# Router of two MoE layers: both halves of the split weights as one 64-column operand, and their sum taken in the turn to token rows

## What is computed

```
scores = sigmoid(x @ router_w.T)                 # f0: 8 columns, top 2 of 8
s      = sigmoid(xf @ Wr.T + br)                 # f1: 32 columns, top 6 of 32
x = x + tanh(g_ffn[0]) * _L0_ffn_ref(_layernorm(x), ...)
x = x + tanh(g_ffn[1]) * _L1_ffn_ref(_layernorm(x), ...)
```

## Time and profile before

| | |
|---|---|
| time, median of 3 | 902.48 us (901.77 to 905.25) |
| the profiled execution | 904.81 us, its span 902.9 us |
| TensorE matmul busy | 875.3 us, 97% of the span |
| VectorE busy | 600.3 us, 66% |
| ScalarE busy | 531.6 us, 59% |
| GpSimd busy | 133.6 us, 15% |
| mean granted TensorE clock | 0.992 |
| router matmuls (L369) | 48, of 8 or 32 stationary and 512 moving columns |
| turns back (L382) | 32 transposes |

### The profile page before, as it was taken

How to read it: one execution, slowest core, us unless ns; L and a number is a source line. 1 busy time by engine, 2 the same in 40 slices (tenths; PEclk the granted TensorE clock), 3 DMA queues, 4 the chain that set the end, 5 groups by cost and what they waited for, 6 DMA issues and landing times.

```text
span 902.9 us, 13884 instructions
## 1 busy us (share of the span) xinstructions
PE 875.3 (97%) x4747; PEld 716.1 (79%) x4768; DVE 600.3 (66%) x1228; ACT 531.6 (59%) x914; POOL 133.6 (15%) x112
## 2 busy tenths in 40 slices
PE   7898999999999999989999999999999999999997
PEld 7898887787788888767777777878788888888886
DVE  4998754466654565589999865658755466565564
ACT  3234343434554354457677767777677867777774
POOL 6996100001002020011121310000000000000000
PEclk9999999999999999999999999999999999999999
DMA  8230151444433442014333244434444344444433
GB/s 283 98 113 29 36 152 34 145 126 133 143 123 101 152 119 69 18 36 124 114 107 104 77 134 134 136 115 140 140 140 143 97 140 140 145 151 151 148 118 105
DMA packets 68389, 106.44 MB, mean 118 GB/s; under 512 B 9120, under 2 KB 31936, under 8 KB 67936
## 3 DMA queue, kind: packets, MB, share of 16 engines
q1 hardware_dynamic: 68112, 105.47, 37.1%
q10 hardware_dynamic: 208, 0.09, 0.0%
HBM read 96.79 MB, written 8.74 MB: 117 GB/s over the span
## 4 chain that ended last, share of the span: by engine, by line
PE 84%; DVE 7%; DMA 3%; POOL 2%; issue 2%; ACT 2%; SPq 1%; DVEq 0%; ACTq 0%; POOLq 0%
PE bank L685 38%; PE bank L721 29%; PE bank L1555 3%; PE bank L1566 2%; PE bank L1546 2%; PE bank L369 1%; PE bank L1458 1%; PE bank L1191 1%; PE bank L1190 1%; PE bank L1188 1%; DMA k_blocks<-k_parts 1%; PE bank L1575 1%; POOL pair_products L1058 1%; PE bank L1209 1%; DVE weighted L1279 1%
## 5 line engine op out<-in xcount | busy, mean ns | idle before, releaser
L482 ACT ACTIVATE y_hi<-y 128x512 fp32r<-128x512 f32 x200 | 124.1, 621 | 81.9 <-DVE y L565 81.2
L579 DVE TENSOR_TENSOR y<-y,gate_rows 128x512 f32<-128x512 f32 x124 | 85.8, 692 | 119.9 <-ACT y L471 118.5
L721 PE MATMUL bank<-y_hi,w_hi 128*128 128x512 f32 x400 | 157.3, 393 | 1.6 <-DVE y_lo L315 1.2
L721 PE MATMUL bank<-y_lo,w_hi 128*128 128x512 f32 x400 | 156.5, 391 | 0.0
L721 PE MATMUL bank<-y_hi,w_lo 128*128 128x512 f32 x400 | 156.0, 390 | 0.0
L315 DVE TENSOR_TENSOR y_lo<-y,y_hi 128x512 fp32r<-128x512 f32 x196 | 134.4, 686 | 29.9 <-ACT y_hi L482 29.6
L465 ACT ACTIVATE activated<-bank 128x512 f32<-128x512 f32 x136 | 81.1, 597 | 80.6 <-PE bank L685 75.8
L685 PE MATMUL bank<-x_hi_first,w_hi 128*128 128x512 f32 x264 | 106.2, 402 | 0.7 <-DVE w_lo L310 0.7
L685 PE MATMUL bank<-x_hi_first,w_lo 128*128 128x512 f32 x264 | 104.2, 395 | 0.0
L685 PE MATMUL bank<-x_lo_first,w_hi 128*128 128x512 f32 x264 | 104.1, 394 | 0.0
L685 PE MATMUL bank<-x_hi_last,w_hi 128*128 128x512 f32 x264 | 104.0, 394 | 0.0
(11 more groups left out here) (156 smaller groups left out, 1368.1 us busy)
## 6 DMA issues: line engine op xcount, KB each, us to landing
gate_rows<-gates SPq DMA_DIRECT2D x156, 256.0 KB, 3.7
w_raw<-in_wu SPq DMA_DIRECT2D x68, 256.0 KB, 2.6
w_raw<-in_wu SPq DMA_DIRECT2D x32, 384.0 KB, 4.1
k_blocks<-k_parts SPq DMA_DIRECT2D x128, 64.0 KB, 2.4
k_parts<-xn_split SPq DMA_DIRECT2D x32, 128.0 KB
v_slot<-in_v_rows SPq DMA_DIRECT2D x16, 256.0 KB, 2.7
ctx_windows<-in_ctx_win SPq DMA_DIRECT2D x3, 1024.0 KB, 13.7
x_mixed<-in_x SPq DMA_DIRECT2D x4, 512.0 KB, 9.3
```

Of the source, the lines that this page charges most:

```text
L482: act.activation(mem.yhi[:, K % S, :], mem.y[:, K % S, :], ACT.Copy).then_inc(s_yh, 1)
L579: dve.tensor_tensor(mem.y[:, K % S, :], mem.y[:, K % S, :], gate, ALU.mult).then_inc(s_yd, 1)
L721: last = pe.matmul(acc(s)[:, c, :], w_[:, Nu % S, wc], y_[:, K % S, :], start=(n == 0 and m == 0), stop=(n == U - 1 and m == 2), skip_grou ...
```

## The change

The router's stationary operand becomes one tile of 64 columns: the upper parts of the weights in columns 0 to 31, the lower parts in columns 32 to 63. For f0, which has 8 experts, the 8 columns are padded with zeros to 32 on the host. `logits_t` then makes four passes a block (x upper and x lower, for both halves of the contraction), so partitions 0 to 31 of the bank hold upper weights x (upper x + lower x), and partitions 32 to 63 lower weights x the same. (The product of both lower parts, left out before, is in it now.) The copy takes 64 partitions. `logits` is no transpose any more: it is a matmul in plain float32 whose moving operand `part_sum` is the 64 x 32 matrix of two identities one above the other (its first 8 columns for f0), which turns the block and adds its two parts at once. `part_sum` is made by one DVE instruction ahead of `constants` and `router_lo` in the convolution stage, with a wait for the identity's load; PE waits for it once.

```diff
-        mem.lts = sb("logits_t", [E1, BLK])
+        mem.lts = sb("logits_t", [LG, BLK])
+        part_sum = sb("part_sum", [LG, EG])
+        s_ps = sem("part_sum_ready")
...
-            rwh = sb(f"rwh{tag}", [P, 2, E], F32R)
-            rwl = sb(f"rwl{tag}", [P, 2, E], F32R)
-            lts = mem.lts[0:E]
+            rws = sb(f"router_split_{tag}", [P, 2, LG], F32R)
+            rwh, rwl = rws[:, :, 0:EG], rws[:, :, EG:LG]
+            lts = mem.lts
...
-                i = 0
                 for c in range(2):
-                    for w_, x_ in ((rwh, mem.xh), (rwh, mem.xl), (rwl, mem.xh)):
-                        last = pe.matmul(dst[0:E, :], w_[:, c, :], x_[m // 2][:, c, tok], start=(i == 0), stop=(i == 5))
-                        i += 1
+                    for x_ in (mem.xh, mem.xl):
+                        last = pe.matmul(dst[0:LG, :], rws[:, c, :], x_[m // 2][:, c, tok],
+                                         start=(c == 0 and x_ is mem.xh), stop=(c == 1 and x_ is mem.xl))
...
-                act.activation(lts, src[0:E, :], ACT.Copy).then_inc(s_lc, 1)
+                act.activation(lts[:], src[0:LG, :], ACT.Copy).then_inc(s_lc, 1)
...
                 pe.wait_ge(s_lc, m + 1)
+                if gated and m == 0:
+                    pe.wait_ge(s_ps, 1)
                 for j in range(BPB):
-                    last = pe.transpose(dst[:, j * E:(j + 1) * E], lts[:, j * P:(j + 1) * P], ident[0:E, 0:E])
+                    last = pe.matmul(dst[:, j * E:(j + 1) * E], lts[:, j * P:(j + 1) * P], part_sum[:, 0:E],
+                                     start=True, stop=True, skip_group_check=True)
...
                         if g == 2 and r == 7:
+                            dve.wait_ge(s_c, 16)
+                            dve.tensor_tensor(part_sum[:], ident[0:LG, 0:EG], ident[0:LG, EG:LG], ALU.add).then_inc(s_ps, 1)
                             f0.constants(dve)
                             f0.router_lo(dve)
```

More of the change, by code:

```diff
@@ L42 @@
 S = 4
+EG, LG = 32, 64
 class Steps:
@@ L82, in build @@
         tg = sb("tg", [P, 4])
-        router = {tag: (sb(f"router_{tag}", [P, 2, E]), sb(f"router_bias_{tag}", [P, E])) for tag, E in (("f0", E0), ("f1", E1))}
+        router = {tag: (sb(f"router_{tag}", [P, 2, EG]), sb(f"router_bias_{tag}", [P, E])) for tag, E in (("f0", E0), ("f1", E1))}
         mhalf = sb("mhalf", [P, NB])
@@ L319, in router_hi @@
                 act.wait_ge(s_rl, 64)
-                act.activation(rwh[:].rearrange("p c e -> p (c e)"), rwf[:].rearrange("p c e -> p (c e)"), ACT.Copy).then_inc(s_rw, 1)
+                act.activation(rwh, rwf[:], ACT.Copy).then_inc(s_rw, 1)
             def router_lo(dve):
                 dve.wait_ge(s_rw, 1)
-                dve.tensor_tensor(rwl[:], rwf[:], rwh[:].bitcast(F32), ALU.subtract).then_inc(s_rw, 1)
+                dve.tensor_tensor(rwl, rwf[:], rwh.bitcast(F32), ALU.subtract).then_inc(s_rw, 1)
             def rows_of(m):
@@ L1847 @@
         "g_x": a["g_xattn"], "g_f": a["g_ffn"], "kpad": kpad, "d_skip": a["L0_xattn_D"],
-        "wu0": np.stack(wu0), "rw0": a["L0_ffn_router_w"].T, "eb0": a["L0_ffn_expert_bias"],
+        "wu0": np.stack(wu0), "rw0": np.pad(a["L0_ffn_router_w"].T, ((0, 0), (0, EG - E0))), "eb0": a["L0_ffn_expert_bias"],
         "wu1": np.stack(wu1), "rw1": a["L1_ffn_Wr"].T, "br1": a["L1_ffn_br"],
```

## The result

The changed kernel took 907.34 us (median of 10, from 902.79 to 910.05), the kernel before beside it 903.45 us (median of 10, from 901.13 to 905.25). The ratio is 1.0036, its interval 1.0022 to 1.0051: 2.0 to 4.6 us slower, in the middle 3.3 us (the two medians by themselves are 3.9 us apart). The forecast had +2.0 us. The profiled execution took 907.17 us, its span 905.4, against 902.9 before.

What follows compares the result with a forecast made beforehand. The prediction took TensorE, without gaps at the router blocks, to bound the kernel. Passes -3.7, turns +5.3 and DVE +0.4 summed to +2.0 us, 904.5 us against the median 902.48, range 900.3 to 907.8.

Steps and rivals of the forecast that it cites:

- What bounds the kernel: All eight router blocks: TensorE has no gap, so work taken off or added there counts nearly in full.
- Two passes less: Eight router blocks, two passes fewer each at 0.230 us: 3.7 us removed, all on the path.
- the passes taken out in the attention stage aren't gained: Rival: in the attention stage the DVE is next in line, 4 passes, 0.9 us lost, 905.4 us; chance 0.05.
- The turn: Transposes become eight load-matmul pairs at 0.11 us: 0.66 us more a turn, 5.3 us for eight turns.
- The DVE, once: Convolution stage: part_sum is held by GpSimd, memset and router_lo follow, weigh starts later: +0.4 us, bounds 0.2 to 1.7.
- the DVE's place costs more: Rival: one more held DVE instruction and a longer PE gap, about +1.5 us on the forecast, 906.0 us; chance 0.08.
- The sum against the median: Whole run: passes -3.7, turns +5.3, DVE +0.4 give +2.0 us; 904.5 us against the median 902.48, +0.2%.
- The signs of being wrong: Wrong if a 64-column pass isn't 0.23 us, a small float32 matmul isn't two pairs, or other stages move over 1 us.
- Unhidden loads: Rival: the turn's loads don't overlap the matmuls, 0.19 us a pair, +7.1 us, 909.6 us; chance 0.10.
- cheap pairs: Rival: the turn's pairs run at the transposes' pace, 0.068 us, sum -0.7 us, 901.8 us; chance 0.17.

Runs made afterwards that it cites:

- the doubled turn: The changed kernel with every matmul of the turn issued twice, 64 pairs more: 913.67 us, ratio 1.0111 to the kernel before.
- the turn alone: The kernel before with only the turn made plain float32 matmuls: 908.04 us, ratio 1.0046; with f0's first means also negated on ACT 905.55 us, 1.0018.
- the same kernel with `part_sum` loaded: The changed kernel with f0's first means negated on ACT and part_sum loaded by a DMA instead of made on DVE: 901.60 us, ratio 0.9990.
- the kernels without the first race: Kernels with f0's first means negated on ACT instead of DVE: before 899.64 us, changed with part_sum loaded 901.60, changed with part_sum on DVE 903.60.
- the run with the sum on DVE: The changed kernel with four transposes of all 64 rows, the two parts added on DVE while copied from PSUM, no part_sum: 898.69 us, ratio 0.9945.
- the changed kernel with the means on ACT: The changed kernel with f0's first means negated on ACT instead of DVE: 903.66 us, ratio 1.0007; a second time 903.60 us, ratio 1.0018.

## Why the prediction was right, and what was off in it

The forecast was 904.5 us against a median of 902.48, +2.0 us in a range of 900.3 to 907.8. Measured were 907.34 us against 903.45, +3.3 us by the ratio. The direction and the largest term were right for the reason given. Another term, the passes, was too large by 0.8 us, which the width of the range covered.

- **What bounds the kernel.** Right for work that is added: the doubled turn cost the run 0.106 us a pair where the trace has 0.113, and the turn alone cost 4.2 us in one comparison and 4.6 to 5.0 in the other where it has 5.1. Wrong in the attention stage for work that is taken off. That PE is busy there for 22.87 of 23 us says that nothing else is ahead of it, and not by how much; the DVE was less than 0.2 us behind.
- **Two passes less.** The price of a pass is right: 0.41 to 0.47 us for two in six blocks, against 0.46, and 64 columns (a load of 134 ns, forecast "about 134") cost no pass any time. But "All of it is on the path" doesn't hold: the two blocks in the attention stage gave 0.12 to 0.13 us each. The term is -2.9 us in place of -3.7. This is the rival *the passes taken out in the attention stage aren't gained*, to which the forecast gave a chance of 0.05, with its mechanism (the DVE is next in line) and nearly its price (0.7 us of the 0.9).
- **The turn.** The term on which the sum hung, and right to 3%: 0.64 us a turn for 0.66. Two records for a plain float32 matmul, the whole load of 128 columns for each, 0.114 us a pair for 0.11. The slope over two load widths gave it. `keep_clock` is no second witness: with its 128 moving columns it takes 0.105 us a pair and the convolution with 180 takes 0.153, so the moving columns explain its pace as well as the load does. What settles it is that pairs with 8 and with 32 moving columns are both 0.114 us apart: (1.05 - 0.255) / 7, and in the attention stage, where eight records take 1.07 us, (1.07 - 0.275) / 7. The 0.05 us for the first load isn't seen by itself. The Trainium skill's figure for float32 (TensorE: Matmul & The Clock Gate, Terms: transpose mode four times faster) would have made a turn some 1.09 us, an estimate by four times the transposes' pace. Here it was 0.98 for 0.34, 2.9 times.
- **The DVE, once.** In the profiled execution right to 0.02 us, with the mechanism as forecast: `part_sum` is held, memset and `router_lo` follow. But the step took a single trace's meeting with GpSimd as the meeting of every run. The rival "the DVE's place costs more" had the right mechanism, one more held instruction, and its price was near: 2.0 us over the same kernel with `part_sum` loaded, in the kernels without the first race. There it isn't a mishap but the rule, in both traces taken.
- **The sum against the median.** +2.6 us by the terms in the two traces, 3.3 in ten runs a side, an interval that reaches down to 2.0: there may be nothing left to explain. What the runs show beyond it: the race at 65.5 us is worth 3 us, and where the DVE isn't held in it, `part_sum` costs 2.0 us in place of 0.4. A mix of the two would lie between +2.6 and +4.0 us if the race went either way equally often in both kernels. How often it does is open: of the six traces of kernels with this instruction on the DVE only that of the run with the sum on DVE has the short `neg_mean`, and there is none like it of the changed kernel itself.
- **The signs of being wrong.** One of them did show: outside the router single waits of PE moved by more than 1 us between the two traces (at 462 and 538 us). They move as much between kernels with the same passes, and what decides them no run asks.
- **The other rivals.** Unhidden loads and cheap pairs are out by the pace of the records, in both engines' rows and in the doubled turn.

## What to carry to other kernels

A matmul that replaces a float32 transpose isn't a transpose with another matrix: it loads its stationary operand twice, at 0.114 us a load in place of 0.068, and with few moving columns that load is its whole price, so fuse a sum into the turn only where the other engine has no room for it. Price such a step by the columns of the stationary operand and by the records, before counting the passes that it saves. Count a saving on a busy engine only up to the point where the next engine is in the way: here two of eight blocks gave a quarter of it. And where two engines exclude each other, a small instruction costs what it meets: read its duration in several traces, and move it to an idle engine before moving anything else past it.

## What the runs showed of the hardware

- A plain float32 matmul with a stationary operand of 64 x 128 and 8 or 32 moving columns is two pairs of load and matmul, 0.113 to 0.114 us apart at a granted clock of 1.00. Loads take 87 ns for 8 columns, 134 for 64 and 188 for 128 in float32r, 187 for 128 in plain float32, and 136 for 128 in a transpose, whose pairs follow each other in 0.068 us.
- A DVE instruction with eight elements a partition, from SBUF to SBUF, took 0.16 or 2.08 us beside a GpSimd instruction of 2.05 us that began within 0.02 us of it. GpSimd waits in the same way: its L1064 takes 1.26 us alone and 1.73 us behind the held DVE instruction. DVE instructions with an input in PSUM (`weigh`, L1279) kept their 0.68 us beside GpSimd's. The Trainium skill names the shared interfaces (GPSIMD Engine Reference, the row on SBUF interfaces: contention with DVE instructions in a 2-port mode or with two SBUF inputs). The traces agree for instructions with two SBUF inputs; `neg_mean` has one, and no trace shows the mode that it ran in. In each case here one of the two engines stood until the other's instruction was done.
- A delay of 1.9 us at 65 us cost the run some 3: behind PE's gap of 2.30 us the granted clock was 0.57 over the window 82 to 86 us, most of it at 1.2 GHz, where without the gap it stayed 1.00. Behind the gap of 1.72 us in the changed kernel with the means on ACT it stayed 1.00 too (81 to 85 us), at 2.4 GHz.
